# Transposing two batches' products and normalised rows with VectorE and the DMA queue in place of TensorE

## What is computed

```python
x = x + attn(layernorm(x))          # 4 x 512 x 512, no softmax in it
#   q, kv = y @ W_q.T, y @ W_kv.T, in 16 heads of 32
#   qf, kvf = fft(q), fft(kv) per head, each divided by its l2 norm
#   kvf = cumsum(kvf, axis=rows);  v = ifft(qf * kvf).real;  result v @ W_o.T
x = x + ffn(layernorm(x))           # hidden width 1536
#   silu((y @ fp8(gate_w)) * gs) * ((y @ fp8(up_w)) * us) @ fp8(down_w) * ds
```

## Time and profile before

| what | value |
|---|---|
| median of 3 runs | 439.82 us (439.19 to 439.83) |
| the profiled execution | 439.65 us |
| its span | 437.8 us |
| PE busy | 425.1 us, 97% of the span |
| DVE busy | 276.2 us, 63% |
| ACT busy | 185.2 us, 42% |
| POOL busy | 104.9 us, 24% |
| DMA queue of SP | 25.77 MB, 18.2% of 16 engines |
| chain that ended last | PE 93%, DMA 2%, POOL 2%, ACT 1%, DVE 1% |

### The profile page before, as it was taken

The page is one execution under the profiler, slowest core; times in us unless marked ns, Lnnn a source line. Parts: engine busy times, 40 slices in busy tenths (PEclk is TensorE's granted clock), DMA queues, the critical chain, the costliest instruction groups (busy, mean ns, idle before and its releaser), DMA issues.

```text
span 437.8 us, 5468 instructions
## 1 busy us (share of the span) xinstructions
PE 425.1 (97%) x1976; PEld 280.2 (64%) x1976; DVE 276.2 (63%) x488; ACT 185.2 (42%) x299; POOL 104.9 (24%) x107
## 2 busy tenths in 40 slices
PE   4999999999999999999999999999999999999995
PEld 4886678745665676665565767666566666555554
DVE  5899889988797882347684571536865754523134
ACT  4958446873434542236432252434523243213130
POOL 0406620011745010400563311400254200400002
PEclk9999999999999999999999999999999999999999
DMA  7993490010240000250000100140000000200002
GB/s 215 328 293 117 141 304 4 0 49 2 72 155 15 1 2 0 85 156 0 2 0 2 49 1 1 47 146 0 0 2 1 1 0 1 96 1 1 0 0 97
DMA packets 17595, 26.14 MB, mean 60 GB/s; under 512 B 1824, under 2 KB 8224, under 8 KB 17568
## 3 DMA queue, kind: packets, MB, share of 16 engines
q1 hardware_dynamic: 17280, 25.77, 18.2%
q10 hardware_dynamic: 288, 0.02, 0.0%
HBM read 21.57 MB, written 4.19 MB: 59 GB/s over the span
## 4 chain that ended last, share of the span: by engine, by line
PE 93%; DMA 2%; POOL 2%; ACT 1%; DVE 1%; issue 0%; SPq 0%; DVEq 0%; POOLq 0%
PE bd L383 20%; PE bg L367 19%; PE bu L367 19%; PE ba L290 15%; PE ba L324 8%; PE bd L290 3%; PE ba L333 1%; PE bd L324 1%; PE ba L303 1%; PE ba L312 1%; DMA hT<-w_q_dram 1%; DMA xTr<-xT_dram 1%; PE bd L276 1%; PE bu L290 1%; PE bg L290 1%; POOL xTs L1350 1%
## 5 line engine op out<-in xcount | busy, mean ns | idle before, releaser
L383 PE MATMUL bd<-dw,fu 128*128 128x512 f32 x376 | 98.6, 406 | 0.0
L367 PE MATMUL bg<-hT,gu 128*128 128x512 f16 x384 | 91.1, 380 | 0.0
L367 PE MATMUL bu<-hT,gu 128*128 128x512 f16 x384 | 90.7, 379 | 0.0
L383 PEld LDWEIGHTS bd<-dw,fu 128*128 128x128 f32 x376 | 69.8, 188 | 16.1
L1046 DVE SCALAR_TENSOR_TENSOR ff<-bu,us,sl 128x512 f32<-128x512 f32 x48 | 35.9, 749 | 61.8 <-PE bu L367 59.8
L290 PE MATMUL ba<-wf,xTs 128*128 128x512 f32 x288 | 69.5, 395 | 0.0
L645 ACT ACTIVATE sl<-bg,gs 128x512 f32<-128x512 f32 x48 | 33.0, 688 | 80.4 <-PE bg L367 80.2
L367 PEld LDWEIGHTS bu<-hT,gu 128*128 128x128 f16 x384 | 37.6, 98 | 45.3
L367 PEld LDWEIGHTS bg<-hT,gu 128*128 128x128 f16 x384 | 34.9, 98 | 44.6 <-issue 8.4
L290 PEld LDWEIGHTS ba<-wf,xTs 128*128 128x128 f32 x288 | 53.7, 188 | 11.8 <-POOL xTs L1350 0.3
L655 ACT ACTIVATE fu<-ff 128x512 fp32r<-128x512 f32 x47 | 29.4, 628 | 55.3 <-PE bd L383 33.9
(11 more groups left out here) (161 smaller groups left out, 474.0 us busy)
## 6 DMA issues: line engine op xcount, KB each, us to landing
h<-x_dram SPq DMA_DIRECT2D x16, 256.0 KB, 3.7
out_dram<-h SPq DMA_DIRECT2D x16, 256.0 KB, 2.3
xTr<-xT_dram SPq DMA_DIRECT2D x12, 256.0 KB, 4.0
hT<-w_q_dram SPq DMA_DIRECT2D x4, 256.0 KB, 4.5
gu<-w_kv_dram SPq DMA_DIRECT2D x4, 256.0 KB, 5.5
h<-xT_dram SPq DMA_DIRECT2D x4, 256.0 KB, 7.5
hT<-gate_w_dram SPq DMA_DIRECT2D x2, 512.0 KB, 6.1
hT<-up_w_dram SPq DMA_DIRECT2D x2, 512.0 KB, 4.9
```

The source lines that it names most:

```text
L367: m = e.matmul(bk[:, :], gu[:, c, 4 * w + k, col:col + P], hT[:, b % 2, part, k, :], start=k == 0 and part == 0, stop=k == KT - 1 and part ...
L383: m = e.matmul(bd[t][:, :], fu_at(n)[:, part, P * t:P * t + P], dw[:, i, :], start=i == 0 and part == 0, stop=i == NI - 1 and part == 1)
```

## The change

For batches 2 and 3 (`b >= TURNED`) PE transposes nothing. DVE transposes 32x32 blocks within the 128 partitions (`dve_zb` for the product, `dve_nb` for the normalised rows) from `qk` into `own`, a buffer that the weights used. SP then moves 32-partition bands back to `qk` in 16 DMAs for each pair of tiles (`sp_zt`, `sp_nt`), so that a whole tile is transposed. ACT and DVE read `qk` from SBUF, where they read a PSUM bank before, with a view that puts the 32-wide pieces in order. The orders of all five programs are new, in the prologue too. Numbers of lines in the changed kernel are larger than in the one before.

```diff
+TURNED = 2
...
         for t in range(NT):
-            order += ([("o", b, t - 1)] if t else []) + [("pT", b, t)] + ([("tri", b, t + 1)] if t < NT - 1 else [])
-        order += [("o", b, 3), ("hT", b, 0), ("hT", b, 1), ("hT", b, 2), ("hT", b, 3)]
+            order += ([("o", b, t - 1)] if t else []) + ([("pT", b, t)] if b < TURNED else [])
+            order += [("tri", b, t + 1)] if t < NT - 1 else []
+        order += [("o", b, 3)] + ([("hT", b, t) for t in range(NT)] if b < TURNED else [])
...
+        def blocks_in(ap):
+            return ap.rearrange("p (k j c) -> p k j c", k=KT, j=4)
+        def blocks_out(ap):
+            return ap.rearrange("p (j k a) -> p k j a", j=4, k=KT)
+        def turned(ap):
+            return ap.rearrange("p (i k a) -> p k i a", i=4, k=KT)
...
         def act_qk(e, b, t, w):
-            if b > 0:
+            if b > TURNED:
+                e.wait_ge(v_hT if w else v_pT, 4 * (b - 1) + t + 1)
+            elif b > 0:
...
         def act_pT(e, b, t):
+                e.wait_ge(d_zt[t // 2], 256 * (b - TURNED + 1))
...
+                e.activation(by_k(pTs[slot][:, 0, :]), turned(qk[:, t, 0, :]), ACT.Copy).then_inc(a_pT, 1)
...
         def act_hT(e, b, t):
+            if b >= TURNED:
+                e.wait_ge(d_nt[t // 2], 256 * (b - TURNED + 1))
+                if t == 0:
+                    e.wait_ge(s_u, NI * (b - 1))
+                e.activation(hT_at(b, 0, t), turned(qk[:, t, 1, :]), ACT.Copy).then_inc(a_hT, 1)
+                return
...
+        def dve_zb(e, b, t):
+            if b == TURNED:
+                e.wait_ge(*rounded(NPR - 1))
+            else:
+                e.wait_ge(d_nt[t // 2], 256 * (b - TURNED))
+            e.wait_ge(p_z, 4 * b + t + 1)
+            e.transpose(blocks_out(own[:, t, :]), blocks_in(qk[:, t, 0, :])).then_inc(v_zb, 1)
+        def dve_nb(e, b, t):
+            e.wait_ge(d_zt[t // 2], 256 * (b - TURNED + 1))
+            e.wait_ge(v_hn, 4 * b + t + 1)
+            e.transpose(blocks_out(own[:, t, :]), blocks_in(qk[:, t, 1, :])).then_inc(v_nb, 1)
...
+        def sp_zt(e, b, u):
+            e.wait_ge(v_zb, 4 * (b - TURNED) + 2 * u + 2)
+            for i in range(4):
+                for j in range(4):
+                    e.dma_start(qk[32 * j:32 * j + 32, 2 * u:2 * u + 2, 0, P * i:P * i + P],
+                                own[32 * i:32 * i + 32, 2 * u:2 * u + 2, P * j:P * j + P]).then_inc(d_zt[u], 16)
+        def sp_nt(e, b, u):
+            e.wait_ge(v_nb, 4 * (b - TURNED) + 2 * u + 2)
...
                 if nxt < NB:
                     pe_qk(e, nxt, 0, 0)
                     pe_qk(e, nxt, 0, 1)
+                pe_down(e, b * NI - 1)
                 pe_gate_up(e, b, 0)
-                pe_down(e, b * NI - 1)
...
             act_center(e, 2)
-            act_first_root(e)
+            act_x(e, 0, 0)
             act_center(e, 3)
-            act_x(e, 0, 0)
```

More of the change, by code:

```diff
@@ L166, in build @@
         d_raw = [[sem(f"d_raw{w}{f}") for f in range(KT)] for w in range(2)]
+        d_zt = [sem(f"d_zt{u}") for u in range(2)]
+        d_nt = [sem(f"d_nt{u}") for u in range(2)]
         d_cst, d_cst2, d_wo, d_sc, d_carry = (sem("d_" + n) for n in ("cst", "cst2", "wo", "sc", "carry"))
@@ L630, in act_hT @@
                     e.wait_ge(*rounded(1))
-                elif b == 1:
+                else:
                     e.wait_ge(*rounded(14))
-                else:
-                    e.wait_ge(s_u, NI * (b - 1))
             e.activation(hT[:, b % 2, 0, :, P * t:P * t + P], src, ACT.Copy).then_inc(a_hT, 1)
@@ L1091, in vector_program @@
             dve_aggr_w(e, 3)
-            dve_one(e)
             dve_aggr_w(e, 4)
@@ L1264, in vector_program @@
                     dve_sum(e, nxt, 1, 1)
+                    dve_sum(e, nxt, 2, 0)
                     dve_stats1(e, nxt, 1)
-                    dve_sum(e, nxt, 2, 0)
+                    dve_stats1(e, nxt, 2)
+                    dve_sum(e, nxt, 2, 1)
+                    dve_sum(e, nxt, 3, 0)
+                    dve_stats1(e, nxt, 3)
+                    dve_sum(e, nxt, 3, 1)
+                    dve_norm_head(e, nxt, range(NT))
+                    dve_norm_tail(e, nxt, range(NT))
+                    dve_scale(e, nxt, 0, 1)
+                dve_f(e, b * NI + 1)
+                if nxt < NB:
+                    dve_scale(e, nxt, 1, 1)
                 dve_f(e, b * NI + 2)
@@ L1325, in vector_program @@
                     dve_hn(e, nxt, 1)
+                    dve_nb(e, nxt, 0)
+                    dve_nb(e, nxt, 1)
+                dve_f(e, b * NI + 9)
                 dve_f(e, b * NI + 10)
+                dve_fu(e, b * NI + 9)
                 if nxt < NB:
                     dve_hn(e, nxt, 2)
-                dve_fu(e, b * NI + 9)
                 dve_fu(e, b * NI + 10)
                 if nxt < NB:
+                    dve_hn(e, nxt, 3)
+                    dve_nb(e, nxt, 2)
+                    dve_nb(e, nxt, 3)
                     dve_hT(e, nxt, 0)
+                    dve_hT(e, nxt, 1)
                 dve_f(e, b * NI + 11)
-                if nxt < NB:
-                    dve_hn(e, nxt, 3)
-                    dve_hT(e, nxt, 1)
-                    dve_hT(e, nxt, 2)
                 dve_fu(e, b * NI + 11)
                 if nxt < NB:
+                    dve_hT(e, nxt, 2)
                     dve_hT(e, nxt, 3)
@@ L1417, in gpsimd_program @@
                     pool_ks(e, nxt, 1)
-                    pool_product(e, nxt, 0)
                 if b + 2 < NB:
@@ L1468, in sp_weights @@
             e.dma_start(stage_at(n), pairs[n][0].rearrange("(k p) n -> p k n", p=P)).then_inc(d_w[n], 16)
+        def sp_zt(e, b, u):
[6 more added lines that the diff above has]
+            e.wait_ge(v_nb, 4 * (b - TURNED) + 2 * u + 2)
+            for i in range(4):
+                for j in range(4):
+                    e.dma_start(qk[32 * j:32 * j + 32, 2 * u:2 * u + 2, 1, P * i:P * i + P],
+                                own[32 * i:32 * i + 32, 2 * u:2 * u + 2, P * j:P * j + P]).then_inc(d_nt[u], 16)
         def sp_out(e, b, t):
@@ L1552, in sync_program @@
                     sp_x(e, nxt, 0)
+                if b + 2 < NB:
+                    sp_xT(e, b + 2, 1)
                 sp_out(e, b - 1, 1)
+                sp_out(e, b - 1, 3)
+                if nxt < NB:
+                    sp_x(e, nxt, 1)
+                sp_out(e, b - 1, 2)
                 if b + 2 < NB:
```

549 lines of the change are left out of this document (274 added, 275 removed).

## The result

The changed kernel takes 470.51 us (median of 4 runs, 467.97 to 472.45), against 439.5 for the kernel before beside it: a ratio of 1.0705, 95% interval 1.0648 to 1.0763. Forecast were 445.1 us and a range of 438.0 to 451.5. The side is right, the size is off by 25 us. The profiled execution took 471.41 us with a span of 469.6, 31.8 more than before.

The account below looks back on a forecast made before the run. The prediction took PE, busy 97% of the span, as the bound. Its sum was 439.65 - 7.0 (transposes) + 11.3 (gate_up waits) + 0.6 (third o) + 0.6 (prologue) = 445.1 us, range 438.0 to 451.5.

Parts of the forecast that it names:

- Removed, -7.0: On PE in batches 2 and 3: 16 groups of four transposes at 0.44 us leave, nothing hides them, -7.0 us.
- The DMA step, 0.50: On SP: each DMA issue in a long row of sixteen takes 0.50 us, with ends 0.37 and 0.51.
- 2.9 and 8.4: Waits in us of the next batch's first gate_up in the second and third loops, for the normalised rows; together +11.3.
- The first pair is half a loop ahead and hidden: In each loop, the first two tiles' products are transposed and moved early enough that PE does not wait.
- The second pair, which I had 0.3 late: In each loop, the last two tiles' products reach the third o 0.3 us late, +0.6 us in all.
- The orders cost nothing: The other moves within the engines' lists were costed at nothing; 1.1 us of idle was all they could win.
- The prologue, +0.6: ACT's input copy x(0, 0), ahead of the last centred weight rows, delays the last folds: +0.6 us, between 0 and 1.7.
- Landing 2.0: The last 32 KB DMA of a row lands 2.0 us after its issue, with ends 1.6 and 3.7.
- the block transpose 0.65: On DVE a 128x512 block transpose takes 0.65 us, ends 0.50 and 1.33; the skill's 1.24 would make the total 447.5.
- Rivals 1 and 2: 1: issues outrun transfers, SP not the bound, 434.5, chance 0.10; 2: step 0.37 to 0.42, 438 to 440, chance 0.12.
- rival 3: Transfers in 512-byte pieces land in 3.7 us instead of 2.0, all four late points move by 1.7: 452 us, chance 0.10.
- the 460 of my own bounds: Total in us with the upper ends: 0.51 an issue, 3.7 landing, 1.33 a transpose, 1.7 for the prologue.

Follow-up runs that it names:

- quarter: The changed kernel with only 4 of each group's 16 DMAs, so its result is incomplete: 437.3 us, 0.9939 of the kernel before.
- probe: The changed kernel with its DMAs put to four other shapes and sources, within SBUF or from DRAM; what lands is not the transposed data: 458.1 us, one run.
- fill: The changed kernel with needless matmuls on PE ahead of the five pieces that wait long: 467.8 us, 1.0634 of the kernel before.
- via_dram: The changed kernel with each group's 16 DMAs replaced by one store to DRAM and four loads, same result: 462.8 us, 1.0526 of the kernel before.
- two_queues: The changed kernel with 8 of the last group's 16 DMAs issued by ACT beside SP: 457.5 us, 1.0378 of the kernel before.

## Why the prediction was right in its side and wrong in its size

Its own steps, against the 26.3 us by which the profiled execution exceeds 445.1:

- **Removed, -7.0:** 5.9 by quarter's busy time, against the pace of 0.44 in the chain: **+1.1**.
- **The DMA step, 0.50: the step of the prediction that failed.** It is 0.64 (0.60 and 0.04), outside my ends of 0.37 and 0.51. All my rows were loads from DRAM, and I set the 2 KB copy within SBUF aside as "not told apart". The trace of the kernel before does tell it apart: ACT issued it in 0.51, longer than the loads' median of 0.39, and probe shows 0.60 within SBUF against 0.42 from DRAM for one shape:

```profile
L613 ACTq DMA_DIRECT2D qk<-qk x9: 504/509/597, 102.5 to 333.5; - x9
```

  In the second loop: o ends at 254.5, SP starts at 259.80 (5.3, forecast 5.25), 31 steps end at 280.7 (20.9, forecast 15.5), gate_up starts at 284.69 (4.0 for landing, copies and subtraction, forecast 3.75). The chain is 30.2 instead of 24.5, and 5.4 of the 5.7 are the issues: 4.3 the step, 1.1 the one long issue. The third loop's is 30.5. The gates wait 8.2 and 12.3 instead of 2.9 and 8.4: **+9.2**. With 0.64 for 0.50 and nothing else changed my sum gives 458 (4.3 more at each gate, 2.1 more at each third o), which is already outside the range; what is left to 471 are the next two points.
- **"The first pair is half a loop ahead and hidden": wrong.** The second tile is transposed only at 217.59, since its product on POOL comes that late, and o asks 11 us later:

```profile
217.59 0.71 DVE L1032 STREAM_TRANSPOSE own<-qk 128x512 f32<-128x512 f32 x1 [1.07 <-POOL qk L1423]
...
231.00 0.69 DVE L1020 TENSOR_TENSOR pT<-qk,pT 128x512 fp32r<-128x512 f32 x1 [3.41 <-ACT pT L638]
```

  I had worked the chain out for the second pair only. It has 10.7 us (218.3 to 229.0, where the two downs ahead of o end). By my own numbers it needed 7.5 + 2.0 + 1.25 = 10.75, so it was never hidden by half a loop but just in time; by the measured step it needs 13.5. The second pair, which I had 0.3 late, had cover enough because all of PE came later. The two first o wait 5.9 where I had 0.6 in all, and that for the third o: **+5.3**.
- **The lower clock behind a wait: not in the sum.** I wrote that PE was at full clock in every slice and took each piece's price from there, also where I forecast PE idle for 8 us. The granted clock over the first o behind its wait, and over wider stretches around the others (third number from the end: 0.50, 0.72, 0.87, 0.76):

```profile
231.90:235.90 4.00, 4.00 (x10) 3.14 (x11) 0.41 (x1) 0.10 (x1) 0.00 (x0) 0.50 0.26 83
...
277.70:290.10 12.40, 5.71 (x19) 2.08 (x17) 2.49 (x4) 3.79 (x7) 1.26 (x1) 0.72 0.12 37
341.50:354.50 13.00, 9.89 (x37) 6.30 (x36) 4.36 (x10) 2.99 (x5) 1.66 (x3) 0.87 0.15 40
383.10:404.00 20.90, 9.09 (x27) 4.58 (x27) 4.71 (x8) 4.19 (x7) 1.26 (x1) 0.76 0.16 46
```

  It makes **+10.3** of busy time. Of it, 4.2 at the first o and behind it were on the path (fill); the 1.8 of the slow down ahead of the second gate ran beside SP's issues and only took the place of waiting. For the rest the path was argued, not shown.
- **The orders cost nothing: nearly.** tri 0.61, `bu` 0.31 and a last down 0.34 wait newly: **+1.3**.
- **The prologue, +0.6:** it went the other way. x(0, 0) landed by 9.80 us, sooner than the 10.7 that my +0.6 implies, and the last centring ended at 11.04 instead of 11.42, ahead of before. I had also overlooked that the first root, with a load of 1.28 us on ACT just ahead of that centring (an ACT_TABLE_LOAD, 9.31 to 10.59 before, at 18.73 now), moved behind it:

```profile
9.80 0.63 ACT L570 ACTIVATE xTs<-h 128x512 fp32r<-128x512 f32 x1 [1.82 <-DMA h<-xT_dram]
10.33 0.71 ACT L564 ACTIVATE hT<-hT,wmv 128x512 f32<-128x512 f32 x1
```

  -0.35 instead of +0.6: **-0.95**.
- **Landing 2.0 and the block transpose 0.65:** 1.9 and 0.65 to 0.71 (two in 1.30 at 258.48), right. The Trainium skill, "VectorE: DVE Perf Modes", "The three transpose paths", has 311 ns for 128x128 in bf16, from which I estimated 1.24; the trace disagrees, 0.71 at most for 128x512 in float32. The 2.4 us that I added to the sum by it counted the gates alone: the products' chain holds two transposes in each loop as well, which would have made it 4.7.

Together 1.1 + 9.2 + 5.3 + 10.3 + 1.3 - 0.95 = 26.25 us.

Rivals 1 and 2 needed a step of 0.23 to 0.42, which was refused by every row of `qk<-own`, 0.585 at the least; rival 3 by the landing. The rule of the Trainium skill behind rival 1 ("DMA: Bandwidth & Descriptors", "Issuing engines are not separate DMA queues": the sequencer's time is usually small beside the DMA's) doesn't hold for these copies, 0.60 to issue and 1.9 to land, and sixteen in a row. That its chance was low was right. The range missed because its upper end took 0.51 for the longest step and had no term for the clock; the 460 of my own bounds was cut off, and it too was too low.

## What to carry to other kernels

Price a chain of DMAs by the number of its issues on one queue, and take an issue's price from a row with the same kind of source and destination: here 0.64 us a step within SBUF and 0.46 to 0.47 from DRAM for the same 32-partition shapes, with 32 KB as with 16, but 3.4 to 3.8 us for four 128-partition loads of 128 KB from DRAM in 512-byte pieces (via_dram). Take it from a row with the same form, if there is one. Work out such a chain for every group that is moved, not only the last one, with the time at which its input is ready. And where a change makes a full TensorE wait for some microseconds, add what the pieces behind the wait take at the lower clock: here 4 us for waits of 6.

## What the runs showed of the hardware

- An SBUF-to-SBUF DMA took 0.59 to 0.60 us to issue, 32 or 16 KB alike, one of the same shape from DRAM 0.42 to 0.43 (probe, medians). Loads of 128 KB from DRAM in 512-byte pieces took 0.52 to 2.03 (via_dram). Two engines issued side by side at 0.65 and 0.66 a step (two_queues).
- Behind 28 of the 30 waits of PE over 2.0 us, in all runs together, the next pieces took 1.3 to 1.9 times as long as their neighbours; where a window lies wholly on such a piece, the granted clock was 0.50, the lower of its two levels (1.2 instead of 2.4 GHz). How long PE had idled doesn't decide it by itself: in two_queues an o behind 2.25 us took 4.58, in probe one behind 2.53 took 3.00, at a granted clock of 1.00. What decides is open.
